# Conv attention: conv bias and row extreme in one VectorE instruction on negated scores, all tap products on GpSimd

## The reference

```python
scores = jnp.einsum('bhqd,bhkd->bhqk', Q, K) / np.sqrt(dh).astype(np.float32)
x = scores.transpose(0, 2, 1, 3).reshape(b * s, h, s)
x = lax.conv_general_dilated(x, conv_w, window_strides=(1,), padding=[(KS // 2, KS // 2)], dimension_numbers=('NCW', 'OIW', 'NCW'))
x = x + conv_b[None, :, None]
scores = x.reshape(b, s, h, s).transpose(0, 2, 1, 3)
weights = jax.nn.softmax(scores, axis=-1)
out = jnp.einsum('bhqk,bhkd->bqhd', weights, V).reshape(b, s, e)
return out @ Wo.T + bo
```

## Time and profile before

| | |
|---|---|
| median of 3 runs | 3880.29 us (3877.61 to 3886.51) |
| profiled execution | 3876.76 us, span 3875.0 us |
| TensorE busy over the span | 3314.4 us (86%) |
| VectorE | 2948.7 us (76%) |
| ScalarE | 2590.8 us (67%) |
| GpSimd | 1805.9 us (47%) |
| costliest group | L2331, 512 maxima, 624.6 us |

### The profile page before, as it was taken

How to read it: one execution, slowest core, us unless ns; L and a number is a source line. 1 busy time by engine, 2 the same in 40 slices (tenths; PEclk the granted TensorE clock), 3 DMA queues, 4 the chain that set the end, 5 groups by cost and what they waited for, 6 DMA issues and landing times. The chain is left out here.

```text
span 3875.0 us, 58774 instructions
## 1 busy us (share of the span) xinstructions
PE 3314.4 (86%) x18963; PEld 2568.7 (66%) x18963; DVE 2948.7 (76%) x5827; ACT 2590.8 (67%) x3859; POOL 1805.9 (47%) x1098
## 2 busy tenths in 40 slices
PE   6867724269999999999999999996888887799999
PEld 4645521146777777777777777774666566799999
DVE  4567889779888888888888989994878787474347
ACT  2334544458888988888888989993667676354443
POOL 0034410016656656565665656661767676260015
PEclk9989956589999999999999999997899898799999
DMA  1046800038888888887888889994559578542224
GB/s 51 0 87 126 152 23 1 1 111 143 151 148 152 153 148 151 147 155 141 157 147 149 157 145 161 163 163 78 95 101 179 105 130 155 171 159 89 75 84 146
DMA packets 1571485, 469.87 MB, mean 121 GB/s; under 512 B 1507318, under 2 KB 1565303, under 8 KB 1569911
## 3 DMA queue, kind: packets, MB, share of 16 engines
q1 hardware_dynamic: 1565047, 449.40, 60.8%
q0 software_dynamic: 6144, 16.79, 1.3%
HBM read 49.00 MB, written 39.58 MB: 23 GB/s over the span
## 5 line engine op out<-in xcount | busy, mean ns | idle before, releaser
L2331 DVE TENSOR_REDUCE d_neg_max<-psum 128x1 f32<-128x1024 f32 x512 | 624.6, 1220 | 161.7 <-PE psum L2066 160.7
L2066 PE MATMUL psum<-d_KH,d_QH 128*128 128x512 f32 x2048 | 685.0, 416 | 25.3 <-DVE d_halves L2340 20.7
L2222 ACT ACTIVATE psum<-psum,d_bias 128x1024 f32<-128x1024 f32 x512 | 558.2, 1090 | 214.7 <-DVE d_bias L2335 205.1
L2340 DVE SCALAR_TENSOR_TENSOR d_halves<-psum,d_halves 128x1024 f16<-128x1024 f32 x512 | 624.3, 1219 | 32.8 <-ACT d_halves L2229 28.2
L2066 PE MATMUL psum<-d_KL,d_QH 128*128 128x512 f32 x2048 | 638.5, 393 | 0.0
L2066 PE MATMUL psum<-d_KH,d_QL 128*128 128x512 f32 x2048 | 636.6, 392 | 0.0
L2022 POOL TENSOR_TENSOR d_KC<-d_KC,d_tap_of 128x1024 f32<-128x1024 f32 x126 | 302.2, 2398 | 536.9 <-ACT d_tap_of L2211 536.9
L2229 ACT ACTIVATE d_halves<-psum 128x1024 f16<-128x1024 f32 x512 | 521.7, 1019 | 3.5
L2066 PEld LDWEIGHTS psum<-d_KH,d_QH 128*128 128x128 f32 x2048 | 356.8, 188 | 172.7 <-issue 69.0
L2066 PEld LDWEIGHTS psum<-d_KL,d_QH 128*128 128x128 f32 x2048 | 385.0, 188 | 87.7
L2066 PEld LDWEIGHTS psum<-d_KH,d_QL 128*128 128x128 f32 x2048 | 385.0, 188 | 87.2
(11 more groups left out here) (542 smaller groups left out, 7479.9 us busy)
## 6 DMA issues: line engine op xcount, KB each, us to landing
f_weights_raw<-in_L_ffn_packed_dram SPq DMA_DIRECT2D x10, 1088.0 KB, 14.8
f_tile<-expert_rows SPq DMA_DIRECT2D x71, 128.0 KB, 2.1
f_expert_out<-f_tile SPq DMA_DIRECT2D x71, 128.0 KB, 1.7
d_probsT<-d_halves SPq DMA_TRANSPOSE x512, 4.3
f_tile<-kept_rows SPq DMA_DIRECT2D x64, 128.0 KB, 2.1
expert_rows<-d_group_mixT SPq DMA_DIRECT2D x7, 1024.0 KB, 11.4
residual_stream<-in_x_dram SPq DMA_DIRECT2D x4, 1024.0 KB, 9.7
kept_rows<-f_tile SPq DMA_DIRECT2D x32, 128.0 KB, 1.7
```

Of the source, the lines that this page charges most:

```text
L2066: last = t.matmul(scores_at(u)[:, cols], q_part[:, ch, j * P:(j + 1) * P], k_part[hh % 2][:, ch, cols], start=k == 0, stop=k == 5)
L2222: a.activation(scores_at(u), scores_at(u), ACT.Exp, bias=bias[u % 2][:, 0:1], accum_out=sums[u // 4 % 4][:, u % 4, :]).then_inc(probs_read ...
L2331: v.tensor_reduce(neg_max[u % 2][:], scores_at(u), AXIS.X, ALU.max, negate=True)\
L2340: v.scalar_tensor_tensor(halves[u % 4][:, 1, :], scores_at(u), LIFT, halves[u % 4][:, 0, :], ALU.mult, ALU.subtract).then_inc(probs_low.se ...
```

## The change

Queries are scaled by -1/4 instead of 1/4, so that the scores come out negated. One VectorE instruction per unit takes the conv bias off them, writes them back to PSUM in place and puts out their minimum; the separate bias column and its counter `bias_ready` are gone. It waits for the exponentials of u - 2 before it, where the bias instruction did. ScalarE takes the exponential with scale -1 and the minimum as bias. ScalarE makes no tap products any more: GpSimd makes all three itself, the two outer ones into `tap_of[:, 0]` and `tap_of[:, 1]`, which both chunks use in turn. The key copies of both chunks stand behind `high_probs` at j = 1 and 2. In `normalize` and `apply` the VectorE instruction becomes a scalar_tensor_tensor with a broadcast second operand.

```diff
@@ add_taps
                         g.tensor_scalar(KC[:, ch, :], K[b % 2][:, ch, 1:S + 1], taps[:, ch, 3 * h + 1:3 * h + 2], 1.0,
                                         ALU.mult, ALU.mult).then_inc(tap_one.sem, 1)
+                        g.wait_ge(tap_two.sem, tap_two.at(seen - 1))
+                        g.tensor_scalar(tap_of[:, 0, :], K[b % 2][:, ch, 0:S], taps[:, ch, 3 * h:3 * h + 1], 1.0,
+                                        ALU.mult, ALU.mult).then_inc(tap_left.sem, 1)
+                        g.wait_ge(tap_three.sem, tap_three.at(at - 1))
+                        g.tensor_scalar(tap_of[:, 1, :], K[b % 2][:, ch, 2:S + 2], taps[:, ch, 3 * h + 2:3 * h + 3],
+                                        1.0, ALU.mult, ALU.mult).then_inc(tap_right.sem, 1)
                         g.wait_ge(tap_one.sem, tap_one.at(seen))
-                        g.wait_ge(tapped.sem, tapped.at(2 * seen - 1))
-                        g.tensor_tensor(KC[:, ch, :], KC[:, ch, :], tap_of[:, ch, :], ALU.add)\
+                        g.wait_ge(tap_left.sem, tap_left.at(seen))
+                        g.tensor_tensor(KC[:, ch, :], KC[:, ch, :], tap_of[:, 0, :], ALU.add)\
                             .then_inc(tap_two.sem, 1)
                         g.wait_ge(tap_two.sem, tap_two.at(seen))
-                        g.wait_ge(tapped.sem, tapped.at(2 * seen))
-                        g.tensor_tensor(KC[:, ch, :], KC[:, ch, :], tap_of[:, ch, :], ALU.add)\
+                        g.wait_ge(tap_right.sem, tap_right.at(seen))
+                        g.tensor_tensor(KC[:, ch, :], KC[:, ch, :], tap_of[:, 1, :], ALU.add)\
                             .then_inc(tap_three.sem, 1)
@@ exps
-                    a.wait_ge(bias_ready.sem, bias_ready.at(u + 1))
+                    a.wait_ge(max_ready.sem, max_ready.at(u + 1))
                     a.wait_ge(inverted.sem, inverted.at(u // 4 - 3))
-                    a.activation(scores_at(u), scores_at(u), ACT.Exp, bias=bias[u % 2][:, 0:1],
+                    a.activation(scores_at(u), scores_at(u), ACT.Exp, bias=neg_max[u % 2][:, 0:1], scale=-1.0,
@@ ScalarE's loop
-                    if j == 0 and hh + 1 < H * B:
-                        tap(hh + 1, 0, 2)
-                    if j in (1, 3) and hh + 1 < H * B:
-                        tap(hh + 1, 1, j - 1)
-                    if j in (2, 5) and hh + 1 < H * B:
-                        high(hh + 1, j // 3)
-                    if j == 6 and hh + 2 < H * B:
-                        tap(hh + 2, 0, 0)
...
                     if u < ALL:
                         high_probs(u)
+                    if j in (1, 2) and hh + 1 < H * B:
+                        high(hh + 1, j - 1)
@@ maximum
-                    v.tensor_reduce(neg_max[u % 2][:], scores_at(u), AXIS.X, ALU.max, negate=True)\
-                        .then_inc(max_ready.sem, 1)
-                    v.wait_ge(max_ready.sem, max_ready.at(u + 1))
                     v.wait_ge(probs_ready.sem, probs_ready.at(u - 1))
-                    v.tensor_scalar(bias[u % 2][:], neg_max[u % 2][:], conv_b[:, h:h + 1], conv_b[:, h:h + 1],
-                                    ALU.subtract, ALU.add).then_inc(bias_ready.sem, 1)
+                    v.tensor_scalar(scores_at(u), scores_at(u), conv_b[:, h:h + 1], None, ALU.subtract, ALU.min,
+                                    accum_out=neg_max[u % 2][:]).then_inc(max_ready.sem, 1)
@@ normalize
-                    v.tensor_tensor(mix[:, tile0:tile0 + 4, h * HD:(h + 1) * HD], group_sum[:],
-                                    inv_sum[:].to_broadcast([P, 4, HD]), ALU.mult).then_inc(normalized.sem, 1)
+                    v.scalar_tensor_tensor(mix[:, tile0:tile0 + 4, h * HD:(h + 1) * HD], group_sum[:], 1.0,
+                                           inv_sum[:].to_broadcast([P, 4, HD]), ALU.mult, ALU.mult)\
+                        .then_inc(normalized.sem, 1)
@@ move_queries
-                    v.tensor_scalar(Q[:, m, half * HALF:(half + 1) * HALF], bank, bq[:, m:m + 1], float(HD) ** -0.5,
+                    v.tensor_scalar(Q[:, m, half * HALF:(half + 1) * HALF], bank, bq[:, m:m + 1], -float(HD) ** -0.5,
@@ apply
-                    v.tensor_scalar(n.xn[:, tile, :], X[:, TB * b + tile, :], n.mv[:, tile, 0:1],
-                                    n.rstd[:, tile:tile + 1], ALU.subtract, ALU.mult).then_inc(n.normed.sem, 1)
+                    v.scalar_tensor_tensor(n.xn[:, tile, :], X[:, TB * b + tile, :], n.mv[:, tile, 0:1],
+                                           n.rstd[:, tile:tile + 1].to_broadcast([P, D]), ALU.subtract, ALU.mult)\
+                        .then_inc(n.normed.sem, 1)
```

More of the change, by code:

```diff
@@ L1884, in stage_conv_attention @@
     biased = c("biased")
-    tapped = c("tapped")
+    tap_left, tap_right = c("tap_left"), c("tap_right")
     tap_one = c("tap_one")
@@ L1893, in stage_conv_attention @@
     max_ready = c("max_ready")
-    bias_ready = c("bias_ready")
     probs_ready = c("probs_ready")
@@ L1932, in stage_conv_attention @@
         v_scale, wo_scale = sb("v_scale", [P, 1], F32), sb("wo_scale", [P, 1], F32)
-        bias = [sb(f"bias{i}", [P, 1], F32) for i in range(2)]
         group_mixT = sb("group_mixT", [P, HALF], F32)
@@ L2201, in _ @@
             def _(a):
-                def tap(hh, ch, k):
-                    b, h = hh // H, hh % H
-                    if h == 0:
-                        a.wait_ge(k_ready.sem, k_ready.at(4 * b + 4))
-                    if k == 0:
-                        a.wait_ge(tap_three.sem, tap_three.at(DC * (hh - 1) + ch + 1))
-                    else:
-                        a.wait_ge(tap_two.sem, tap_two.at(DC * (hh - 1) + ch + 1))
-                    a.activation(tap_of[:, ch, :], K[b % 2][:, ch, k:S + k], ACT.Copy,
-                                 scale=taps[:, ch, 3 * h + k:3 * h + k + 1]).then_inc(tapped.sem, 1)
                 def high(hh, ch):
@@ L2286, in _ @@
                     queries(0, j)
-                tap(1, 0, 0)
                 a.wait_ge(v_scaled.sem, v_scaled.at(5))
@@ L2492, in stage_conv_attention @@
     first_taps.passed(2 * DC)
-    tapped.passed(2 * DC * (H * B - 1))
-    for k in (tap_one, tap_two):
+    for k in (tap_one, tap_left, tap_right, tap_two):
         k.passed(DC * (H * B - 1))
@@ L2503, in stage_conv_attention @@
         k.passed(2 * B)
-    for k in (scored, max_ready, bias_ready, probs_ready, probs_high, probs_low):
+    for k in (scored, max_ready, probs_ready, probs_high, probs_low):
         k.passed(ALL)
```

## The result

The changed kernel takes 3849.98 us (median of 4, 3848.98 to 3863.66) against 3878.95 for the kernel before on the same chip: a ratio of 0.993 with an interval of 0.9911 to 0.9949, that is 20 to 35 us faster. The prediction was 3884 us, no change in effect, with a range from 3850 to 3918. On a second chip the same kernel came to 0.9958 (0.9941 to 0.9974), 16 us.

A forecast was written before the change was run, and what follows sets the result against it. TensorE, 98% busy, was taken as the bound. Terms -10 - 6 + 8 + 10 + 2 = +4 us on the profiled 3876.8 us, which lay 3.5 below the median, gave 3884 us, range 3850 to 3918.

The forecast's parts named there:

- What bounds the stage: From 866 to 2640 us TensorE is the bound, 98% busy; shorter paths elsewhere pay only where it stands still.
- the ceiling of 55 us: TensorE's lateness and waits in the stage: all that this change can win, about 55 us, 1.4%.
- Maximum and bias in one: Fused VectorE instruction per unit: 1.28 to 1.33 us, saving 0.11 to 0.16 us of VectorE and 0.23 us of latency.
- Steady stalls, -10: Heads without fills: the 0.4 us stall before the second unit shrinks to 0.1; with stalls behind ScalarE's taps, -10 us.
- The moved norm tiles, -6: Moved norm tiles, turned tiles and their exponentials come 0.3 us earlier on ScalarE: -6 us.
- The price of the sets, +18: 24 applies and 24 later low queries wait for GpSimd, +0.7 to +1.0 us each: +8 and +10 us of time.
- The start, +2: First units of the stage, where low queries are on TensorE's path and GpSimd had pauses: +2 us.
- GpSimd's cover: GpSimd makes all taps in 21.2 of 25.7 us per head, 5 us of cover, so no new key waits.
- ScalarE's share: Sign to look for: ScalarE at about 72% busy in the stage after losing its tap products.
- "Faster": Rival, chance 0.30: two-input VectorE instructions slip into GpSimd's gaps, the sets cost nothing, 3856 us.
- "VectorE becomes the bound": Rival, chance 0.25: a slow fused instruction or product waits lift VectorE's head work past TensorE's 25.7 us, 3920 us.
- the 1 us in the mean: Sign of a slower outcome: the product by the inverse sums going over 1 us in the mean.

The follow-up runs named there:

- the furthest experiment: Changed kernel with inverse sums in PSUM and low queries from a one-SBUF-input tensor_scalar, their low part left out: 3838.39 us, 0.9859 of the kernel before.
- the fused kernel: Kernel before with only the fused bias and minimum; ScalarE's taps and the old forms of apply and product kept: 3868.46 us, 0.9947.
- taps-only run: Changed kernel with maximum and bias as two instructions again; GpSimd makes all taps, new forms of apply and product kept: 3921.32 us, 1.0086.
- the one-input form: Low queries by an accumulating tensor_scalar, low part left out, inverse sums in PSUM: 3838.39 us with taps on GpSimd, 3849.32 with two of three on ScalarE.
- the second trace: The changed kernel, unaltered, run again on a second chip: 3871.74 us, 0.9958 of the kernel before.

## Why the prediction was wrong

*What bounds the stage* held. TensorE is at 98% still, and the gain came out of its stalls. Of the ceiling of 55 us the change took 16 to 27; the furthest experiment (0.9859) took 55 by the ratio and 43 by the units, with the low part of the queries left out.

*Maximum and bias in one* was mis-sized. Predicted were 1.28 to 1.33 us of VectorE; the instruction is listed at 1.288 but the next starts after 1.21, so 0.24 us per unit is saved, not 0.11 to 0.16. ScalarE gains 0.18, not 0.23. The searches of the earlier trace rows misled because one search is followed there by another, which starts 0.12 after the read; here the read lies beside an instruction of another kind. Per head the error is 8 x 0.1 = 0.8 us of VectorE, and with it a head's VectorE work falls by 1.9 us. The right value was the lower bound that I had named, the reduction's 1.21.

*Steady stalls, -10.* A plain head fell from 26.0 to 25.3 us, not from 25.9 to 25.7. The last batch alone gives -7.8 us. This term was too small by the same mis-sizing, since in the fused kernel it is already 25.5. (ScalarE's tap products stood in four units of a head, and with the moved key copies six come earlier, not five.)

*The moved norm tiles, -6:* 5.8 us of waits became 0.8. Right; each part of the change alone gives some of it (3.3 left with the fusion, 2.2 with the taps).

*The price of the sets, +18.* A set is the eight applies, or the eight low queries, of one batch. The mechanism is there, at about half the price per instruction: the applies have +0.41 us (870 for 456 ns) and the 24 later low queries +0.40, where I took +0.7 to +1.0. The rows of those 24, before and changed (1250 to 2300 us):

```profile
L2368 DVE TENSOR_TENSOR d_QL<-d_ln_xn,d_QH 128x256 fp32r<-128x256 f32 x24 | 10.1, 421 | 0.0
...
L2352 DVE TENSOR_TENSOR d_QL<-d_ln_xn,d_QH 128x256 fp32r<-128x256 f32 x24 | 19.7, 819 | 0.0
```

Of the applies 12 of 24 waited (1.14 to 1.38 us), of these low queries 9 of 24 (0.88 to 2.41); the others kept their short time. The conversion into time failed as well. In the third batch heads 3 and 4 cost 0.6 us instead of 2.7, and heads 15 and 0 give 1.0 back instead of costing 3.3. I had weighed the waits of a set against 3 us of spare VectorE time, where the fusion adds 1.9 us a head to that. The taps-only run shows 5 to 6 us per set without it. I had priced the halves of the change one by one and added them up; that is the step that failed: +18 us for the sets, where the changed kernel's trace has, at these heads, under 1 us a set of applies and -1.0 a set of low queries. How much of the difference is the halved price and how much the added room, no run separates. The waits of the low queries do cost something still: with the product out of the way, the one-input form gains 11.7 us by the units with the taps on GpSimd and 6.9 with ScalarE's, so that the move of the taps makes them dearer by some 5 us, where I had +10 and +2.

*The start, +2:* heads 0 and 1 of the first batch took 58.3 us and take 54.3 (55.2 in the second trace). The sign of this term was wrong. The fusion alone gives 57.3 and the taps alone 57.2, so it is no one part's.

*Put at nothing:* the heads 1 of the later batches, where the mix of the batch before is turned and projected. They grow by 2.5, 0.9 and 1.0 us, some 1.6 of the 2.5 by the clock at 0.50. TensorE waits there for the moved mix (L2107 for L2250, 5.4 us in all where it was 3.8) and for the products (L2119 for L2338, 3.5 where it was 2.3). With the inverse sums in PSUM these heads are 0.8 us shorter than before, so that it is the waiting product again.

*GpSimd's cover* held: 21.57 of 26 us busy (16.66 in the earlier trace rows), 77% in the stage as said, and ScalarE waits 0.3 us for keys in all. ScalarE's share is 76%, not 72: its busy time fell by 215 us, 0.86 per tap product and not the 1.146 listed. The listed durations overlap (in the kernel before one tap product is listed from 1607.74 for 1.14 us and the next instruction starts at 1608.79), which explains a part of it.

*Left out:* the form of the apply. I priced it by its two inputs alone, as a cost. It is one in duration (0.47 for 0.40 us), and it is worth some 17 us by who goes first beside a 2.4 us sum: with the old form the changed kernel would have shown no change, close to the predicted time, but not for the reasons given. The trace of before has only applies that went first (401 to 621 ns), three of them 88 to 90 ns ahead of a sum; it could not show what happens with less lead.

*The rivals.* "Faster" had the right sign and nearly the size (3856), but its condition, that the two-input instructions slip into gaps, held for 27 of the 48 only: 21 waited, and the stage bore it. So its nearness is partly luck. "VectorE becomes the bound" was put at 3920; its own terms (3884 + 25 + 18) add up to 3927. The taps alone gave 3921, which is near either, by stalls of which an estimated third is the clock, so that this nearness too is partly luck. The product L2338 stayed under the 1 us in the mean that I had named as its sign.

## What to carry to other kernels

Where one part of a change makes an engine shorter and another makes it wait, sum them on that engine head by head before turning either into time: here -20 and +33 us apart made -16 to -27 together. Where VectorE must run beside a busy GpSimd, look for the instructions with two SBUF inputs and put the small operand in PSUM: 725 ns became 222. A stall of a few us is worth more than its length if the clock falls behind it: an estimated 3 of 6.2 us here.

## What the runs showed of the hardware

- The accumulator read behind a fused tensor_scalar (0.14 us) lies beside the next VectorE instruction: start to start 1.21 us for 1024 float32 elements from PSUM to PSUM.
- A tensor_scalar with one large SBUF input and no accumulator waits for GpSimd too, and at leads at which a scalar_tensor_tensor with two goes first: it (128x256) lost to a sum in 13 of 13 places at 70 to 87 ns and won in 5 of 5 at 88 to 92; scalar_tensor_tensor (128x256) won in 30 of 30 at 64 to 82 ns.
- An accumulating tensor_scalar from SBUF to SBUF never waited (401 to 422 ns in 32), nor did an instruction with one SBUF and one PSUM input (221 to 223 ns in 128), each in a kernel whose GpSimd makes all taps (77% busy in the changed kernel).
- After 5.01 us of idle time TensorE was granted 0.50 for the next 5 us. A pair of 512-column float32 matmuls started every 0.85 us there and every 0.46 at the full clock.
